# Third chunk of queries, keys and outputs as one 128-column product, in a two-layer cross-attention kernel on one core

## What is computed

```
q = heads(x @ Wq.T)
out = attend(q, text @ Wk.T, text @ Wv.T) + attend(q, ip @ Wk_ip.T, ip @ Wv_ip.T)
x = out @ Wo.T + bo + x
```

```
q = heads(x @ W_q);  probs = softmax(q @ k_text / 4)
qsem = l2norm(probs @ text);  sem = qsem @ l2norm(ip).T
probs_ip = softmax(q @ k_ip / 4 + 0.5 * sem) * mask
out = (probs @ v_text + probs_ip @ v_ip) @ W_out + b_out + x
```

## Time and profile before

| | |
|---|---|
| median of 3 runs | 808.63 us (806.24 to 812.35) |
| span of the profiled execution | 803.6 us |
| busy | PE 766.8, PEld 622.5, DVE 561.2, ACT 426.2, POOL 402.3 us |
| units of layer 0, steady | 37.5 us each (scores of units 7 and 8 begin at 320.6 and 358.0) |
| units of layer 1, steady | 55.1 us each |
| tail after the last background work | from 689 us on |

### The profile page before, as it was taken

One profiled execution on the slowest core, in us unless ns is written; L12 is line 12 of the kernel. 1 busy time (PEld: TensorE's weight loads), 2 busy tenths in 40 slices (PEclk: granted clock), 3 DMA queues, 4 the chain that ended last, 5 costly groups with the idle time before them and its releaser, 6 DMA issues.

```text
span 803.6 us, 17120 instructions
## 1 busy us (share of the span) xinstructions
PE 766.8 (95%) x6342; PEld 622.5 (77%) x6342; DVE 561.2 (70%) x1535; ACT 426.2 (53%) x915; POOL 402.3 (50%) x297
## 2 busy tenths in 40 slices
PE   5889999999999999999999999999999999988896
PEld 5777788888888878887877787788887887766574
DVE  4457575757567575858768788688697787686745
ACT  5244646364637464556465565555654655455551
POOL 5521312020202040405678877778769768779763
PEclk9999999999999999999999999999999999999999
DMA  8975736663738373835263345163172442400010
GB/s 280 243 191 156 173 112 170 206 169 120 184 98 222 106 191 93 224 88 150 71 167 101 86 127 156 41 170 104 51 188 70 109 127 61 118 1 19 18 33 17
DMA packets 102514, 100.66 MB, mean 125 GB/s; under 512 B 9752, under 2 KB 101664, under 8 KB 102432
## 3 DMA queue, kind: packets, MB, share of 16 engines
q1 hardware_dynamic: 101952, 99.24, 44.6%
q10 hardware_dynamic: 480, 0.33, 0.2%
HBM read 61.65 MB, written 36.74 MB: 122 GB/s over the span
## 4 chain that ended last, share of the span: by engine, by line
PE 78%; DVE 7%; issue 4%; POOL 3%; ACT 3%; DMA 3%; SPq 1%; POOLq 0%; DVEq 0%; ACTq 0%
PE pB L385 23%; PE pB L504 13%; PE pB L467 8%; PE pB L490 7%; PE pB L588 5%; PE pPV L531 4%; PE pPV L526 4%; PE pPV L536 4%; PE pB L545 3%; PE pPV L522 3%; POOL Y L1318 2%; DVE m_sb L1069 2%; DMA P<-in_Wki 1%; DMA KP<-k0d 1%; DVE m_sb L1067 1%
## 5 line engine op out<-in xcount | busy, mean ns | idle before, releaser
L1318 POOL TENSOR_TENSOR Y<-P,wv 128x512 f32<-128x512 f32 x120 | 156.2, 1319 | 107.2 <-ACT P L861 107.0
L1084 DVE TENSOR_TENSOR Y<-pB,Y 128x512 f32<-128x512 f32 x160 | 108.9, 686 | 70.6 <-PE pB L504 60.7
L467 PE MATMUL pB<-KP,QP 96*128 96x256 f32 x640 | 129.6, 288 | 3.6 <-DMA KP<-k0d 2.2
L1295 POOL TENSOR_TENSOR klo<-xin,khi 128x256 fp32r<-128x256 f32 x18 | 13.2, 756 | 227.0 <-ACT khi L772 227.0
L467 PEld LDWEIGHTS pB<-KP,QP 96*128 96x128 f32 x640 | 106.1, 190 | 17.7 <-issue 6.7
L1069 DVE TENSOR_REDUCE m_sb<-pB 128x2 f32<-128x504 f32 x160 | 108.0, 676 | 11.4 <-PE pB L467 9.6
L490 PE MATMUL pB<-QP,KP 100*128 100x512 f32 x320 | 109.1, 421 | 3.3 <-DMA QP<-mlo 2.7
L861 ACT ACTIVATE P<-pB 128x512 f32<-128x512 f32 x160 | 86.5, 596 | 39.7 <-PE pB L490 29.8
L861 ACT ACTIVATE P<-pB,ln 128x512 f32<-128x512 f32 x160 | 101.2, 691 | 0.0
L851 ACT ACTIVATE wv<-pB 128x512 fp32r<-128x512 f32 x120 | 66.8, 591 | 56.5 <-PE pB L490 55.1
L772 ACT ACTIVATE Vs<-pPV 128x512 f32<-128x512 f32 (+1 forms) x80 | 39.4, 492 | 102.0 <-PE pPV L526 68.7
(11 more groups left out here) (180 smaller groups left out, 1692.0 us busy)
## 6 DMA issues: line engine op xcount, KB each, us to landing
QP<-q0d SPq DMA_DIRECT2D x64, 192.0 KB, 4.1
KP<-k0d SPq DMA_DIRECT2D x64, 192.0 KB, 4.3
c_sb<-in_cT SPq DMA_DIRECT2D x16, 512.0 KB, 5.0
q0d<-qhi SPq DMA_DIRECT2D x32, 256.0 KB, 2.5
k0d<-khi SPq DMA_DIRECT2D x32, 256.0 KB, 2.5
q0d<-qlo SPq DMA_DIRECT2D x16, 256.0 KB, 3.0
k0d<-klo SPq DMA_DIRECT2D x16, 256.0 KB, 2.7
VB<-vipd SPq DMA_DIRECT2D x6, 640.0 KB, 3.9
```

What stands on the lines that cost most here:

```text
L467: made = mm(bank[:, sc * S:sc * S + S], QP[i][0:KROWS, j, a, sc * 128:sc * 128 + 128], KP[i][0:KROWS, j, :], start=True, stop=True)
L1084: tt(Y[:, p, dst, :], bank_of["gp", q, dst][:, :], Y[:, p, dst, :], MUL).then_inc(dv_y, 1)
L1318: tt(Y[:, p, ch, :], P[:, p, ch, :], PH[q % HR][ch].bitcast(F32), SUB).then_inc(po_y, 1)
```

## The change

The weights of queries, keys and outputs now stand as `[128, k, 640]`: the high columns at 0 to 319, the low columns of chunk 2 right behind them at 320 to 383, those of chunks 0 and 1 from 384 on. So 256 to 383 holds the high and the low columns of chunk 2 side by side. One product with these 128 stationary columns writes high by high into rows 0 to 63 of the bank and low by high into rows 64 to 127; high by low goes, with 64 columns, to rows 0 to 63. Qb has 5 products (3 of 128 columns, 2 of 64), Kb 8 (4 and 4), output part 1 of units 0 to 13 has 5.

VectorE adds the upper half: for Qb and Kb it writes source less high part into a new tile `half` and then adds rows 64 to 127 of the bank (two operations, the second waits for the first); for the output it follows its addition of bias and residual with a second addition.

Splits of wq, wo and wki are in two column pieces each. `image_values` (twice, in the last two units) has 4 products for each k instead of 3. `repeat(12)` takes two banks, and its middle third (four steps) is two products of 64 rows and 256 columns each. `ones` lies in another tile. `SIZE`, `PACE` and `FIRST` follow the smaller jobs: a unit has 104 background products in layer 0 (111 before), 101 in layer 1 (108 before).

```diff
-SIZE = {"Qa": 16, "Qb": 8, "Kt": 12, "KT": 3, "Ka": 24, "Kb": 12, ...}
-PACE = ((14, 14, 13, 12, 12, 11, 10, 10, 9, 6), (13, 13, 12, 12, 12, 11, 11, 10, 8, 6))
-FIRST = (14, 14, 14, 14, 14, 5, 2, 2, 2, 30)
+SIZE = {"Qa": 16, "Qb": 5, "Kt": 12, "KT": 3, "Ka": 24, "Kb": 8, ...}
+PACE = ((13, 13, 12, 12, 11, 11, 10, 9, 8, 5), (12, 12, 12, 11, 11, 11, 10, 9, 8, 5))
+FIRST = (14, 14, 14, 14, 14, 5, 2, 2, 2, 23)
...
+            def both(W, k):
+                return W[:, k, 2 * 128:2 * 128 + 128]
+            def stacked320(W, hi, lo):
+                out = []
+                for k in range(2):
+                    out += [(both(W, k), hi[:, k, 0:S]), (W[:, k, high_columns(2)], lo[:, k, 0:S])]
+                return out + [(both(W, 2), hi[:, 2, 0:S])]
+            def stacked512(W, ts):
+                out = []
+                for k in range(EC):
+                    pair = [(both(W, k), chi[:, k, ts]), (W[:, k, high_columns(2)], clo[:, k, ts])]
+                    out += pair if k < EC - 1 else pair[::-1]
+                return out
...
             def repeat(n):
-                bank = take("idle", n)
-                for _ in range(n):
-                    mm(bank[:, :], wki[:, 0, 0, 0:128], wki[:, 0, 1:3, 0:256], start=True, stop=True)
+                banks = [take("idle", i) for i in range(2)]
+                for i in range(n):
+                    if n // 3 <= i < 2 * n // 3:
+                        for h, bank in enumerate(banks):
+                            rows = slice(64 * h, 64 * h + 64)
+                            mm(bank[:, 0:S], wki[rows, 0, 0:128], wki[rows, 1, 0:S], start=True, stop=True)
...
+            def stacked_low(u, job, out, bank, hi, at):
+                if u:
+                    dv.wait_ge(dv_bg, low_no(u, job) - 1)
+                then(low(half[0:64, at], bank[0:64, at], hi))
+                settled()
+                tt(out, half[0:64, at], bank[64:128, at], ADD).then_inc(dv_bg, 1)
...
+                if part == 1 and u < U - 2:
+                    then(made)
+                    settled()
+                    made = tt(dst, dst, bank[64:128, 0:S], ADD)
                 made.then_inc(dv_op, 1)
```

More of the change, by code:

```diff
@@ L235, in build @@
         ST = sb("ST", [128, 2, H, 6])
+        ones = ST[:, :, :, :].rearrange("p c h r -> p (c h r)")[:, 0:128]
+        half = sb("half", [128, S])
         cs = sb("cs", [128, 2 * EC * B * NIP])
@@ L384, in chain @@
                 for n, (l, r) in enumerate(pairs):
-                    made = mm(out, l, r, start=(n == 0), stop=(n == len(pairs) - 1))
+                    rows = out if len(l.shape) == 2 and l.shape[1] == out.shape[0] or len(l.shape) == 3 else out[0:l.shape[1]]
+                    made = mm(rows, l, r, start=(n == 0), stop=(n == len(pairs) - 1))
                     if signal is not None and n == len(pairs) - 1:
@@ L408, in prepare @@
                     pe.wait_ge(lo_x, 3 * (u + 1))
-                    for n, m in enumerate(chunks):
-                        yield from chain(bank[0:CHUNK[m], n * S:n * S + S], pairs320(wq, 128 * m, CHUNK[m], khi, klo),
-                                         pe_bg if m == chunks[-1] else None)
+                    if part == 1:
+                        yield from chain(bank[:, 0:S], stacked320(wq, khi, klo), pe_bg)
+                    else:
+                        for n, m in enumerate(chunks):
+                            yield from chain(bank[:, n * S:n * S + S], pairs320(wq, m, khi, klo),
+                                             pe_bg if m == chunks[-1] else None)
                     give(bank)
@@ L426, in prepare @@
                     lo = 0 if L else TXT0 - 1
[L427 to L430 removed]
+                    if part == 1:
+                        yield from chain(bank[:, lo:S], stacked512(wki, slice(lo, S)), pe_bg)
+                    else:
+                        for n, m in enumerate(chunks):
+                            yield from chain(bank[:, n * S + lo:n * S + S],
+                                             keys512(wki, m, slice(lo, S)),
+                                             pe_bg if m == chunks[-1] else None)
                     give(bank)
@@ L449, in prepare @@
                     ts = slice(128 * ch, 128 * ch + 128)
-                    yield from chain(bank[:, 0:C], [(c, v) for v, c in pairs512(w, slice(0, C), ts)], pe_bg)
+                    yield from chain(bank[:, 0:C], [(c, v) for v, c in pairs512(w, ts)], pe_bg)
                     give(bank)
@@ L583, in output @@
                     pe.wait_ge(ac_mb, closing_no(u))
+                if part == 1 and u < U - 2:
+                    for _ in chain(bank[:, 0:S], stacked320(wo, ahi, alo), pe_op):
+                        pass
+                    give(bank)
+                    return
                 for n, m in enumerate(PARTS[part]):
                     M = CHUNK[m]
-                    pairs = pairs320(wo, 128 * m, M, ahi, alo)
+                    pairs = pairs320(wo, m, ahi, alo)
                     for k, (l, r) in enumerate(pairs):
@@ L634, in image_tokens @@
                     pe.wait_ge(dv_set, 3)
-                    mm(bank[:, 0:128], ones[:, :], cs[:, 128:256], start=True, stop=True).then_inc(pe_ip, 1)
+                    mm(bank[:, 0:128], ones, cs[:, 128:256], start=True, stop=True).then_inc(pe_ip, 1)
                     give(bank)
@@ L1213, in image_values @@
                 made.then_inc(dv_bd, 1)
[L1215 removed]
+            nc.vector.memset(ones, 1.0)
             nc.vector.memset(ln2[:, :], float(np.log(2.0)))
```

89 lines of the change are left out of this document (58 added, 31 removed).

## The result

The changed kernel takes 832.47 us (median of 4 runs, 830.90 to 835.16) against 809.97 for the kernel before in the same comparison (4 runs, 806.24 to 812.35): ratio 1.029, 95% interval 1.026 to 1.032. It is 22.5 us slower. The forecast was 804.7 us with a range of 795 to 812 and .10 for slower: it was wrong in size and in sign.

The account below looks back on a forecast made before the run. TensorE was taken as the bound in both layers. 13.2 us saved, less 2.8, 2.1, 3.0, 1.2 and .4, left 3.7, taken as 3.9: span 799.7, time 804.7 us, range 795 to 812.

Parts of the forecast that it names:

- What the removed products are worth: TensorE's products saved in Qb, output part 1 and Kb of both layers: 5.3, 4.7, 3.6 and 1.8, together 15.4 us.
- rival of the alternating widths: Each alternation of 128 and 64 columns costs .07 us, 16 us in all, giving 821 us; chance .02.
- The added operations: VectorE's 46 additions at .44 us each, 20 us, laid beside TensorE's work except at four places.
- Place 1: Layer 0, pair 1, maximum in pB5: TensorE waits .6 us behind Qb's half and addition; 2.8 us over units 1 to 5.
- Place 2: Boundaries of layer 0's units: less work over the keys' load chain, each gives back .3 us; seven boundaries, 2.1 us.
- Place 3: Layer 1, pair 4, Kb's low parts: TensorE waits about 1.0 us instead of .5; 3.0 us over units 8 to 13.
- Place 4: Pair 9, units 9 to 12: output's addition moves the context's split past GpSimd's start; .3 x 4 = 1.2 us.
- blocking rival: VectorE and GpSimd block each other in layer 1, some 3.2 us a unit, 19 in six, giving 819 us; chance .08.
- The start: Units 0 and 1, before the steady state: 1.1 us of savings worth nothing, VectorE's four extra jobs cost .6 in all.
- mechanism of "slower": VectorE and GpSimd blocking each other in layer 1; a net loss from 1.4 us a unit on; chance .08.

Follow-up runs that it names:

- e8: e7 with the start's waits filled: 20 wide idle products, 11 more ahead of the first shift and of unit 1's first scores; 804.5 us, .995 of before.
- e11: e8 run again, unchanged, on another chip: 803.4 us, .991 of the kernel before.
- e12: e8 with output part 1 stacked in layer 0 only, plain in units 8 to 13: 801.0 us, .988 of the kernel before.
- e3: Changed kernel with Qb's low part moved back behind the third piece of background products in layer 0: 820.6 us, 1.017 of the kernel before.
- e4: Changed kernel with output part 1 as before (8 products of 64 columns, no addition): 819.2 us, 1.015 of the kernel before.
- e7: Changed kernel with context split before output part 1 (units 9-12), Qb's (layer 0) and Kb's (layer 1) low parts behind the third piece: 807.4 us, .998 of before.
- e1: Changed kernel with the 12 idle products of before (128 rows, 512 columns, one bank): 829.4 us, 1.024 of the kernel before.

## Why the prediction was wrong

- *What the removed products are worth* (15.4 us gross): held as a mechanism. The products of Qb in the changed kernel's timeline, ending ahead of a maximum, step by .12 and .11 us whether they have 64 or 128 columns:

```profile
149.06 0.28 PE L399 MATMUL pB<-klo,wq 128*64 128x256 f32 x1
...
149.18 0.28 PE L399 MATMUL pB<-khi,wq 128*128 128x256 f32 x1
149.29 0.41 PE L511 MATMUL pB<-KP,QP 96*128 96x256 f32 x2
```

  With the orders repaired and the start filled, 3.9 us (e8), 7.1 (e11) and 9.6 (e12) of it reached the median. The rival of the alternating widths (and the drain of the Trainium skill's page "TensorEngine Tiling (Array Packing)", section "Key Properties") showed in none of these rows.
- *The added operations*: .42 us each, against .44 taken.
- *Place 1* (2.8 us): the wait came where it was forecast, in units 1 to 5, .61 to .68 us in the first four against .6. By e3 it cost .8 to 1.1 us in units 2 and 3, where .55 was taken. What failed is the question of what else moves with it. The split of wq follows Qb's low part in VectorE's program; in unit 5 it made the wait 1.95 us. That cost some 1.7 us, and 4.6 where the clock fell behind it, as in one of four traces; .55 was forecast.
- *Place 2* (2.1 us): the size fits one unit, but the waits that were to show it aren't there. Unit 3 takes 36.8 us in e3 where 37.4 less .88 is 36.5, .3 given back against .3 forecast; but there is no wait for the keys in that unit. The forecast wait of .3 at each boundary didn't come: the changed kernel has .12 in unit 2, .28 in unit 4, and no more. What the .3 of unit 3 is stays open, and that it agrees is luck. The tail was missing: late landings of 2.0 to 2.6 us in e4 and e11, each with a clock stretch of 7 us.
- *Place 3* (3.0 us): forecast was a wait of 1.0 us in units 8 to 13. It was none in unit 8, 1.39 in unit 9 and .71 in each of units 10 to 13. Putting the order right (e7) gave back 1.2 us in unit 9 and under .2 in each of the others, since another wait took its place: the wait was there, its price was too high.
- *Place 4* (1.2 us) is the first term that failed, by a factor of ten: 12.4 us. I had the addition pushing the split past GpSimd's start, and priced it at .3, with one subtraction (1.0) as the bound. The row of klo<-kip shows what one such operation pays, and there were four in a row. The bound should have been 4 x 1.2 each unit; 3.1 was measured. The prediction's own signs of this showed: clo operations of over .63 us (1.45), units of layer 1 of over 56 us (58.2), and a wait in another pair, pair 9. The blocking rival said "one subtraction" too, and reached 819.
- *The start* (put at +.9 in all) is the second: 10.3 us in the trace. I priced the waits but not what TensorE's clock does behind them. Before had three waits of 1.6 to 2.1 us in its first 90 us with the clock up in its profile; in the changed kernel they are 2.9 to 3.3. How much of the 10.3 any execution pays varies, from 2.8 to all of it in the unfilled variants; e8, with these waits filled, is .7 us behind before at unit 2. What made the second wait 2.9 us in every unfilled variant was not taken apart.
- *The chances*: the mechanism of "slower" had .08 and needed a loss of 1.4 us a unit; it came to 3.1 in four units. The range ended below it.

## What to carry to other kernels

Where an operation with two SBUF inputs runs beside a stream of GpSimd operations, its cost depends on when in a GpSimd operation it comes: .14 to 1.29 us here for one of 64x4 elements (.45 in the changed kernel, where it came .4 us before the subtraction's end), 2.5 or 5.8 for a row of four. An added operation of .4 us ahead of it decides which: price the whole row at its blocked duration before calling it hidden, and put such rows ahead of the new work. Where TensorE's work is taken away ahead of a wait that is already 1.5 to 2 us, the saving can turn into a stretch at half clock that costs more than the work did; look for every such wait before shortening what covers it. And when the completion of a job moves, everything that follows it in the same list moves too: check each of them.

## What the runs showed of the hardware that I had not expected

- The granted clock fell behind waits of 1.4 to 2.9 us in some executions and not in others (in the kernel before 2.03 and 2.39 us without, 2.01 us with a fall; 1.36 us with a fall in e1, 2.92 without in e4), and each fall lasted some 3.5 or 7 us.
- Four VectorE operations against a queue of GpSimd subtractions didn't run in one gap once GpSimd was ahead (5.79 us at 547.53); they alternated one to one, 1.45 us each.
- Eight idle products of 64 rows and 256 columns, which go in turn to the upper and the lower half of the rows, began every .083 us (27.67 to 28.34), where products of 128 rows and 256 columns step by .12.
